# Window attention of a two-layer transformer: scores per head on 64x64 quarters of TensorE, two blocks of queries stacked per tile

## The chip, the cores and the metric

One core of a Trainium2 chip runs the whole program. The metric is device time in microseconds (us) of one execution. TensorE multiplies matrices (in the profile PE is its matmuls and PEld its weight loads), VectorE (DVE) and ScalarE (ACT) do elementwise work and read PSUM, GpSimd (POOL) does elementwise work on SBUF, and SyncE (SP) starts most transfers. Every engine runs its own queue in order; semaphores connect the queues.

## The reference

Two transformer layers with modulated norms over x of shape (4, 1024, 128). Each has an attention and a routed mixture of experts. The change is in the attention of the first layer: 16 heads of size 64, q and k with an RMS norm over all heads, a bias that is linear in the distance, and a causal window of 64 keys back.

```python
q = rmsnorm(x @ wq.T, q_norm_w); k = rmsnorm(x @ wk.T, k_norm_w); v = x @ wv.T   # split into 16 heads of 64
scores = einsum('bhqd,bhkd->bhqk', q, k) * HD ** (-0.5)
scores = scores + slopes[:, None, None] * dist               # dist = key position - query position
causal = (dist > 0) | (dist < -WINDOW)                       # WINDOW = 64
weights = softmax(where(causal, -inf, scores))
out = einsum('bhqk,bhkd->bhqd', weights, v) @ wo.T
...
h = layernorm(x) * (1 + ca) + sa                             # six modulation vectors for each batch element
x = x + ga * attention(h, ...)
h = layernorm(x) * (1 + cb) + sb
x = x + gb * experts(h, ...)
```

## The kernel before

The program goes through stages one after the other, with a barrier between them: `start_stage` (norm of x, modulation), `rms_stage`, `window_attention_stage` (the first layer's attention, with the routing of the experts for the first three batch elements woven in), `route_last_stage`, the first layer's experts, and then the second layer.

The attention works on pairs of heads: 4 batch elements with 8 pairs each make 32 pairs (`HP`). Queries come in blocks of 64 (`BLK`), so 1024 tokens are 16 blocks (`NBLK`), and each block of queries sees 128 keys: its own block and the one ahead of it. A group is four blocks, so a pair has four groups (`GRP`) and the stage 128 (`G`). All of it is float32. TensorE's 32-bit matmuls stand in the trace as two records each, each with its own weight load.

For the pair after the one that is being worked on, six units make q (units 0 and 1), k (2 and 3) and v (4 and 5), each of 512 tokens (`project`, L714 and L717), into two PSUM banks that alternate. They are copied out by ACT: k to `k_pad` (L824), v to `v_tiles` (L826). Of q, ACT writes head 0's half (L819) and DVE head 1's half (L892) into a block-diagonal `q_bd`: per block a 128x128 square with the two heads' queries on the diagonal and zeros elsewhere. The v tiles are also moved by 64 rows with two SP transfers into `v_shift`, since odd blocks begin at half a tile.

For each group, in order: one 128x128 matmul a block makes the scores of both heads, partitions 0 to 63 for one and 64 to 127 for the other (L734); DVE adds the bias and takes the minimum of the negated scores (L960); ACT takes the exponential and its row sum (L869), DVE inverts the sums (L966), POOL multiplies (L989), TensorE transposes (L745), DVE copies the result out (L972), TensorE multiplies with v, 128 rows by 64 columns of the array for each head (`o_ps`, L760), and ACT copies that out (L877). After the four groups of a pair, eight matmuls add its part of the output projection (`wo_ps`, L773). Two score banks alternate by group.

TensorE's order in step g is written out by hand: the scores of group g; the units of the next pair that fall into this step; the transposes of group g-2; the product of group g-3; every fourth step the output projection. The other engines have loops of their own over g, and the norms, logits, softmax and ranks of the router are hung in at fixed places within a batch element (the constants `STATS1` to `PREFIX`, counted in groups).

`start_stage` also makes six modulation vectors for each layer and batch element as rows, stores them to DRAM and loads them back into all partitions as `mod_rows` (P, 2, B, 6, D).

Of the kernel before, what the change touches and what calls it, by code (L numbers as in the profile page):

```python
# [21 lines left out]
P = 128  # L22
# [14 lines left out]
RMS_EPS = 1e-6  # L37

# [12 lines left out]
STATS1, HAT1, MODULATE, HAT2, TURN0, TURN1, LOGITS, SOFTMAX, PREFIX = 6, 9, 11, 16, 18, 19, 22, 23, 30  # L51
# [13 lines left out]
SA, CA, GA, SB, CB, GB = range(6)  # L65

# [122 lines left out]
def double_norm_stage(nc, K, A, name, layer, scale, shift, arrays, before=None):  # L189
# [3 lines left out]
    with ExitStack() as st:  # L193
# [9 lines left out]
        with nc.Block() as block:  # L203
# [7 lines left out]
            def _(dve):  # L211
# [9 lines left out]
                def modulate(b):  # L221

                    if b >= B:
# [4 lines left out]
                    nc.vector.tensor_tensor(h, h, bc(K.mod_rows[:, layer, b, scale, :], 1, TPB), ALU.mult  # L228
# [3 lines left out]
                                            bc(K.mod_rows[:, layer, b, shift, :], 1, TPB), ALU.add  # L232
# [48 lines left out]
def start_stage(nc, K, A, gram):  # L281
# [4 lines left out]
    rows_dram = nc.dram_tensor("mod_rows_dram", [2 * B * 6 * D], F32, kind="Internal").ap()  # L286
    with ExitStack() as st:
# [24 lines left out]
        with nc.Block() as block:  # L312
            @block.sync
            def _(sp):
# [10 lines left out]
                sp.dma_start(rows_dram.rearrange("(l b n) -> b l n", l=2, b=B), rows[:]).then_inc(rows_stored, 16)  # L325
# [242 lines left out]
def window_attention_stage(nc, K, A, gram, hq, hk, M, N1, N2, aff_in):  # L568
# [3 lines left out]
    with ExitStack() as st:  # L572
# [4 lines left out]
        nbias = K.sb("nbias", [P, PAIRS, P], ctx=st)  # L577
# [3 lines left out]
        qbd = K.sb("q_bd", [P, 2, NBLK, P], ctx=st)  # L581
# [14 lines left out]
        def fill(pool):  # L596

            for n, dst in enumerate((qbd[:].rearrange("p a b c -> p (a b c)"), kk[:, :, 0:BLK], vs[0:BLK, :, 0, :])):
                nc.gpsimd.memset(dst, 0.0).then_inc(filled, 1)
                pool.wait_ge(filled, n + 1)  # L600
            nc.gpsimd.memset(zero[:], 0.0).then_inc(filled, 1)
# [9 lines left out]
        def scale_q(dve):  # L611
# [19 lines left out]
        op = K.ps("o_ps", [P, 4, BLK], st)  # L631
        wp = [K.ps(f"wo_ps{i}", [P, CPT, D], st) for i in range(2)]
        (h_in, p_mm, a_out, q_out, v_sh0, v_sh1, s_mm, biased, exped, rsum, normed, turned, pt_out, pv_mm, o_out,
         wo_mm, wo_gated, x_added, prob_set, scaled, shifted) = K.sems(
            st, "win", "h_in", "proj_mm", "act_out", "q_out", "v_shift_even", "v_shift_odd", "score_mm", "biased",
            "exp", "rsum", "normed", "turned", "probsT_out", "pv_mm", "o_out", "wo_mm", "wo_gated", "x_added", "probs_set",
            "scaled", "shifted")
        v_sh = (v_sh0, v_sh1)
        GRP = NBLK // 4
        HP = B * PAIRS  # L640
        G = HP * GRP
        PER = GRP * PAIRS
        extra = {PER * (b + 1) + at: (b, what) for b in range(B - 1)
                 for at, what in ((TURN0, "turn0"), (TURN1, "turn1"), (LOGITS, "logits"), (PREFIX, "prefix"))}
        units = [(0, u) for u in range(6)]
        steps = []
        for g in range(G):
            h, start = g // GRP + 1, len(units)
            if h < HP:
                units += [(h, u) for u in ((0, 1), (2, 3), (4,), (5,))[g % GRP]]  # L650
            if g in extra:
                units.append(extra[g])
            steps.append(range(start, len(units)))
        place = {unit: n for n, unit in enumerate(units)}

        def unit_steps(g):

            return steps[g] if g < G else []

# [9 lines left out]
        with nc.Block() as block:  # L669
            @block.tensor  # L670
            def _(pe):
# [24 lines left out]
                def project(n):  # L696
# [3 lines left out]
                    if n >= 2:  # L700

                        hh, uu = units[n - 2]
                        pe.wait_ge(a_out, n - 1)
                        if uu in (0, 1):
                            pe.wait_ge(q_out, 2 * hh + uu + 1)
# [15 lines left out]

                for n in range(6):
                    project(n)
                for g in range(G + 4):
                    h, r = divmod(g, GRP)
                    if g < G:
                        if r == 0:
                            pe.wait_ge(a_out, out_count(h, 3))
                            pe.wait_ge(q_out, 2 * h + 2)
                        if g >= 2:  # L730
                            pe.wait_ge(biased, g - 1)
# [4 lines left out]
                        m.then_inc(s_mm, 1)  # L736
                    for n in unit_steps(g):
                        project(n)
                    if 2 <= g < G + 2:
                        k = g - 2  # L740
                        pe.wait_ge(normed, k + 1)
                        if k >= 1:
                            pe.wait_ge(pt_out, k)
                        for i in range(4):
                            m = nc.tensor.transpose(tp[:, i, :], pr[:, k % 3, i, :], K.ident[:])  # L745
                        m.then_inc(turned, 1)
                    if 3 <= g < G + 3:
                        k = g - 3
                        hh, rr = divmod(k, GRP)
                        pe.wait_ge(pt_out, k + 1)  # L750
                        if rr == 0:
                            pe.wait_ge(a_out, out_count(hh, 5))
                            pe.wait_ge(v_sh[hh % 2], 32 * (hh // 2 + 1))
# [1809 lines left out]
```

## Time and profile before

| | us |
|---|---|
| median of 3 runs | 2059.05 |
| lowest and highest | 2058.75 and 2061.07 |
| span of the profiled execution | 2056.4 |
| TensorE busy in it | 1579.5 |
| DVE busy | 1339.0 |
| ACT busy | 1135.7 |
| POOL busy | 550.2 |

The median lies 2.65 us above the span of the profiled execution. The busy times are sums over stages with different limits, so each stage is read by itself. In a timeline, records of the same kind that follow each other are merged: "x8" are eight records, and the next row's start tells when the following work began. A matmul's end is modelled, so the pace of TensorE is read from starts.

### The profile page before, as it was taken

The numbers are of one execution on the slowest core, as the hardware profiler recorded it, in microseconds if no ns is written. First come the engines' busy times: TensorE is split into PE (matmuls) and PEld (weight loads), VectorE is DVE, ScalarE is ACT, GpSimd is POOL, SyncE is SP. The second block draws the span as 40 slices with busy tenths as digits, with TensorE's granted clock in tenths as the row PEclk, the third lists the DMA queues.
The fourth block names the chain that finished last, engine by engine and source line by source line (L and its number), as shares of the span: only waits on it lengthen the run. The fifth ranks groups of instructions, "written<-read, shape, count | busy, mean of one in ns | idle before, by whom it ended". The sixth has DMA issues, their size and how long they took to land. (4 is left out here: it accounts for less than half of the span.)

```text
span 2056.4 us, 34421 instructions
## 1 busy us (share of the span) xinstructions
PE 1579.5 (77%) x11512; PEld 917.7 (45%) x11512; DVE 1339.0 (65%) x3318; ACT 1135.7 (55%) x2965; POOL 550.2 (27%) x615
## 2 busy tenths in 40 slices
PE   6799999999991699245999999999999735424910
PEld 3478777777771699221222222222222234323910
DVE  5655656656564322267999999999999287842523
ACT  3366766666651344142688888888888733111300
POOL 2133323524526400571001001001000020372056
PEclk9799999999995799666899999999999967556965
DMA  5144311211101676142000000000000000013832
GB/s 191 39 156 156 107 30 36 54 28 43 42 21 37 203 234 205 52 122 83 23 21 26 18 26 18 27 18 26 19 25 2 1 0 6 21 45 124 253 91 72
DMA packets 86203, 138.99 MB, mean 68 GB/s; under 512 B 18084, under 2 KB 57252, under 8 KB 85900
## 3 DMA queue, kind: packets, MB, share of 16 engines
q1 hardware_dynamic: 62860, 92.08, 15.2%
q0 software_dynamic: 11936, 34.49, 5.1%
q10 hardware_dynamic: 11232, 10.23, 1.4%
q8 instruction: 93, 1.52, 0.3%
q14 instruction: 82, 0.67, 0.1%
HBM read 75.51 MB, written 45.11 MB: 59 GB/s over the span
## 5 line engine op out<-in xcount | busy, mean ns | idle before, releaser
L2062 DVE TENSOR_REDUCE q_max<-s_ps 128x1 f32<-128x1024 f32 x512 | 598.2, 1219 | 14.0 <-PE s_ps L1953 6.8
L2043 ACT ACTIVATE probs<-s_ps 128x512 f32<-128x512 f32 x1024 | 535.5, 603 | 124.5 <-PE s_ps L1974 124.3
L1953 PE MATMUL s_ps<-k_stack,q_stack 64*128 64x512 bf16 x1024 | 351.2, 397 | 16.9 <-PEq L96 8.5
L1974 PE MATMUL s_ps<-q_stack,k_stack 64*128 64x512 bf16 x1024 | 319.5, 384 | 20.2 <-ACT probs L2043 15.8
L1988 PE MATMUL o_ps<-probs,v_aug 128*32 128x512 f32 x2048 | 273.6, 606 | 0.7 <-ACT probs L2043 0.7
L1974 PEld LDWEIGHTS s_ps<-q_stack,k_stack 64*128 64x128 bf16 x1024 | 78.6, 94 | 333.9 <-ACT probs L2043 281.9
L989 POOL TENSOR_TENSOR probs<-probs,p_rsum 128x512 f32<-128x512 f32 x128 | 132.9, 1038 | 325.8 <-DVE p_rsum L966 325.1
L869 ACT ACTIVATE probs<-s_biased,s_min 128x128 f32<-128x128 f32 (+1 forms) x512 | 197.7, 391 | 37.0 <-DVE s_min L960 35.6
L734 PE MATMUL score_ps<-k_pad,q_bd 128*128 128x128 f32 x1024 | 146.7, 287 | 0.0
L960 DVE CUSTOM_DVE_ANT_0 s_biased<-score_ps,nbias 128x128 f32<-128x128 f32 (+1 forms) x512 | 115.8, 282 | 41.8 <-PE score_ps L734 40.6
L1580 POOL CAST neg_max_parts<-neg_max 16x128 bf16<-16x128 f32 x32 | 9.0, 281 | 474.7 <-DVE neg_max L2070 474.7
L734 PEld LDWEIGHTS score_ps<-k_pad,q_bd 128*128 128x128 f32 x1024 | 125.9, 194 | 7.4 <-issue 1.0
L1953 PEld LDWEIGHTS s_ps<-k_stack,q_stack 64*128 64x128 bf16 x1024 | 77.5, 94 | 113.2 <-DVE q_max L2062 104.3
L892 DVE TENSOR_SCALAR q_bd<-proj_ps,qscale 64x512 f32<-64x512 f32 x64 | 48.4, 756 | 107.9 <-PE proj_ps L714 104.7
L1474 ACT ACTIVATE moe0b_hid<-moe0b_hps,moe0b_wblock 128x256 f32<-128x256 f32 x156 | 66.9, 473 | 82.5 <-PE moe0b_hps L1429 80.7
L972 DVE COPY probsT<-probsT_ps 128x512 f32<-128x512 f32 x128 | 86.7, 677 | 37.0 <-PE probsT_ps L745 36.4
L1619 POOL DMA_INDIRECT moe0g_yg<-moe_rows,moe_slot x64 | 66.4, 1038 | 157.9 <-POOLq L96 139.0
L869 ACT ACTIVATION_READ_ACCUMULATOR probs<-s_biased,s_min 128x1 f32 x512 | 98.0, 191 | 0.0
L1538 POOL DMA_INDIRECT moe1g_yg<-moe_rows,moe_slot x64 | 61.2, 956 | 121.3 <-PEq L1533 102.1
L819 ACT ACTIVATE q_bd<-proj_ps,qscale 64x512 f32<-64x512 f32 x64 | 43.7, 683 | 84.9 <-PE proj_ps L714 84.8
L1498 DVE TENSOR_TENSOR moe0b_y<-moe0b_yps,moe0b_wblock 128x256 f32<-128x256 f32 x39 | 16.6, 425 | 99.6 <-PE moe0b_yps L1439 99.6
L760 PE MATMUL o_ps<-probsT,v_shift 128*64 128x64 f32 x1024 | 73.5, 235 | 8.8 <-ACT oT L877 8.6
(315 smaller groups left out, 2824.5 us busy)
## 6 DMA issues: line engine op xcount, KB each, us to landing
moe0b_wblock<-in_L_ffn_blocks SPq DMA_DIRECT2D x39, 578.0 KB, 3.9
moe_rows<-zero_rows POOLq DMA_DIRECT2D x18, 960.0 KB, 4.4
moe1b_wblock<-in_L_ffn_blocks SPq DMA_DIRECT2D x39, 256.0 KB, 3.5
v_shift<-v_tiles SPq DMA_DIRECT2D x32, 256.0 KB, 3.1
v_shift<-v_tiles SPq DMA_DIRECT2D x32, 224.0 KB, 3.6
qk_parts_dram<-qk_parts SPq DMA_DIRECT2D x16, 384.0 KB, 2.7
q_stack<-qk_parts_dram SPq DMA_DIRECT2D x192, 32.0 KB
k_stack<-qk_parts_dram SPq DMA_DIRECT2D x192, 32.0 KB
```

What stands on the lines that cost most here:

```text
L734: m = nc.tensor.matmul(sp_[g % 2][:, i, :], qbd[:, h % 2, j, :], kk[:, h % 2, BLK * j:BLK * j + P], start=True, stop=True)
L760: m = nc.tensor.matmul(op[a * BLK:(a + 1) * BLK, i, :], src[:, a * HD0:(a + 1) * HD0], pt[:, k % 2, i, a * BLK:(a + 1) * BLK], start=True, ...
L869: r = nc.scalar.activation(pr[:, g % 3, i, own], sb_[:, g % 2, i, own], ACT.Exp, scale=-1.0, bias=mn[:, g % 4, i:i + 1], accum_out=sm[:, g ...
L960: q = v.tensor_tensor_reduce(sb_[:, g % 2, i, own], sp_[g % 2][:, i, own], nbias[:, h % PAIRS, own], 1.0, 3e38, ALU.add, ALU.min, mn[:, g ...
L972: v.tensor_copy(pt[:, k % 2], tp[:]).then_inc(pt_out, 1)
L989: nc.gpsimd.tensor_tensor(pb, pb, bc(ri[:, g % 4, :], 2, P), ALU.mult).then_inc(normed, 1)
L1474: nc.scalar.activation(hid[:, j % 2, f, :], hp[n % 4][:, 0:BR], gelu, bias=bias).then_inc(g_out, 1)
L1953: mm = nc.tensor.matmul(s1[u % 2][:, c * CH:(c + 1) * CH], qs[head_rows(m), quad % 4, j, qt * P:(qt + 1) * P], ks[head_rows(m), quad % 4, ...
L1974: nc.tensor.matmul(bank_of("exp", 4 * k + pos)[:], ks[head_rows(m), quad % 4, j, kt * P:(kt + 1) * P], qs[head_rows(m), quad % 4, j, half ...
L1988: m = nc.tensor.matmul(op[32 * h:32 * h + 32, :], va[:, quad % 2, kt, h, :], pr[:, k % 2, h, :], start=(kt == 0), stop=(kt == TPB - 1))
L2043: nc.scalar.activation(pr[:, k % 2, HEADS[pos], :], bank_of("exp", n)[:], ACT.Exp).then_inc(sm["exp"], 1)
L2062: v.tensor_reduce(mx[:, h % 4, col:col + 1], s1[u % 2][:], AX.X, ALU.max).then_inc(sm["maxed"], 1)
```

## The change

- Scores: `q_bd` is replaced by `q_rows`, q of both heads as it comes (128 rows, 1024 columns a pair). A block's score of one head is a matmul of 64 rows by 64 columns of the array, which are the quarters (row half a = the head, column half e = even or odd block). Bank a now holds head a alone, with an even block on partitions 0 to 63 and the odd one on 64 to 127.
- Steps: a step is eight blocks, with both banks; a pair has two steps (`HALVES`), the stage 64 (`S`). Transposes, probabilities and copies keep their size (four tiles of 128x128) but belong to one head; there are two a step, g = 2n and 2n+1. The product of a step is taken at once, for both heads (`o_ps` has 512 columns). Units come three in each step.
- ACT writes q out alone, 128 partitions at a time; DVE's half is gone, and its clearing of `probs` too. The first block of each sequence has no block ahead of it: its 64 columns get FAR added by two small matmuls for each head (`outside`).
- Buffers: `probs` has four in place of three, `probsT` four in place of two; the bias is kept for all 16 heads on all partitions (1024 KB in place of 512 KB).
- `mod_rows` keeps four kinds of rows out of six (from GA on).
- The router's prefix is placed two groups earlier.

```diff
+ROW0 = GA
-    rows_dram = nc.dram_tensor("mod_rows_dram", [2 * B * 6 * D], F32, kind="Internal").ap()
+    rows_dram = nc.dram_tensor("mod_rows_dram", [2 * B * (6 - ROW0) * D], F32, kind="Internal").ap()
...
-        nbias = K.sb("nbias", [P, PAIRS, P], ctx=st)
+        nbias = K.sb("nbias", [P, H0, P], ctx=st)
-        qbd = K.sb("q_bd", [P, 2, NBLK, P], ctx=st)
+        qq = K.sb("q_rows", [P, 2, T], ctx=st)
+        outside = K.sb("outside", [P, BLK], ctx=st)
...
-        pr = K.sb("probs", [P, 3, 4, P], ctx=st)
+        pr = K.sb("probs", [P, 4, 4, P], ctx=st)
-        pt = K.sb("probsT", [P, 2, 4, P], ctx=st)
+        pt = K.sb("probsT", [P, 4, 4, P], ctx=st)
-        op = K.ps("o_ps", [P, 4, BLK], st)
+        op = K.ps("o_ps", [P, 8, BLK], st)
...
-                units += [(h, u) for u in ((0, 1), (2, 3), (4,), (5,))[g % GRP]]
+                units += [(h, u) for u in ((0, 1, 2), (3, 4, 5))[n % HALVES]]
...
+                def scores(n):
+                    h, r = divmod(n, HALVES)
+                    if r == 0:
+                        pe.wait_ge(a_out, out_count(h, 3))
...
+                    if n >= 1:
+                        pe.wait_ge(biased, 2 * n)
+                    for i in range(4):
+                        edge = r == 0 and i == 0
+                        for e, a in ((0, 0), (1, 1), (1, 0), (0, 1)):
+                            j, rows = 8 * r + 2 * i + e, slice(a * BLK, (a + 1) * BLK)
+                            m = nc.tensor.matmul(sp_[a][e * BLK:(e + 1) * BLK, i, :],
+                                                 qq[rows, h % 2, BLK * j:BLK * (j + 1)],
+                                                 kk[rows, h % 2, BLK * j:BLK * j + P],
+                                                 start=True, stop=not (edge and e == 0))
+                        if edge:
+                            for a in range(2):
+                                rows = slice(a * BLK, (a + 1) * BLK)
+                                m = nc.tensor.matmul(sp_[a][0:BLK, 0, 0:BLK], M.ones[rows, 0:BLK], outside[rows, :],
+                                                     start=False, stop=True)
+                    m.then_inc(s_mm, 1)
...
-                for g in range(G + 4):
-                        for i in range(4):
-                            j = 4 * r + i
-                            m = nc.tensor.matmul(sp_[g % 2][:, i, :], qbd[:, h % 2, j, :],
-                                                 kk[:, h % 2, BLK * j:BLK * j + P], start=True, stop=True)
...
+                for n in range(S + 3):
+                    mine = list(own(n))
+                    if n < S:
+                        scores(n)
+                    for k in mine[:2]:
+                        project(k)
+                    if 1 <= n < S + 1:
+                        turn(2 * (n - 1))
+                    if 2 <= n < S + 2:
+                        product(n - 2)
+                    for k in mine[2:]:
+                        project(k)
+                    if 1 <= n < S + 1:
+                        turn(2 * (n - 1) + 1)
+                    if n >= 4 and n % HALVES == 0:
+                        output_product((n - 4) // HALVES)
+                    for k in extra(n):
+                        project(k)
...
             @block.scalar
...
+                for n in range(S + 2):
+                    mine = list(own(n))
+                    for k in mine[:1]:
+                        evacuate(k)
+                    if n < S:
+                        exponentials(2 * n)
+                    for k in mine[1:2]:
+                        evacuate(k)
+                    if n < S:
+                        exponentials(2 * n + 1)
+                    for k in mine[2:]:
+                        evacuate(k)
...
+                    if n >= 2:
+                        output(n - 2)
...
             @block.vector
...
-                    v.tensor_scalar(qbd[BLK:P, h % 2, u * 8:u * 8 + 8, BLK:P],
-                                    pj[n % 2][BLK:P, :].rearrange("p (j q) -> p j q", q=BLK),
-                                    qs[BLK:P, h % PAIRS:h % PAIRS + 1], None, ALU.mult).then_inc(q_out, 1)
...
+                for n in range(S + 1):
+                    if n < S:
+                        bias(2 * n)
+                        bias(2 * n + 1)
+                    if n >= 1:
+                        turned_out(2 * (n - 1))
+                    if n < S:
+                        invert(2 * n)
+                    if n >= 1:
+                        turned_out(2 * (n - 1) + 1)
+                    if n < S:
+                        invert(2 * n + 1)
+                    routed(2 * n)
+                    routed(2 * n + 1)
```

## Rows read from the trace of the kernel before

**Rows 1.** Windows, first to last pair's scores: us; PE, PEld, DVE, ACT, POOL busy; PEclk; DMA.
```profile
87.10:597.20 510.10, 493.88 (x4723) 399.84 (x4722) 306.70 (x1507) 350.76 (x1344) 193.85 (x182) 0.99 0.23 71
```
**Rows 2.** Waits in 87 to 618 us: line, releaser, us in total, times, longest.
```profile
PE o_ps L760 <- ACT oT L877: 8.6, 28, 0.7
PE proj_ps L680 <- issue: 6.3, 3, 2.1
```
**Rows 3.** Timeline of PE (start, us, line): first and last pair's first scores.
```profile
87.10 1.05 PE L734 MATMUL score_ps<-k_pad,q_bd 128*128 128x128 f32 x8
...
597.20 1.06 PE L734 MATMUL score_ps<-k_pad,q_bd 128*128 128x128 f32 x8
```
**Rows 4.** Timeline of PE, each kind of work of one pair.
```profile
331.49 1.16 PE L734 MATMUL score_ps<-k_pad,q_bd 128*128 128x128 f32 x8
332.48 1.88 PE L714 MATMUL proj_ps<-hk,wkT 128*128 128x512 f32 x4
334.20 0.60 PE L745 MATMUL probsT_ps<-ident,probs 128*128 128x128 f32 x4
334.73 0.33 PE L760 MATMUL o_ps<-probsT,v_shift 128*64 128x64 f32 x4
334.89 0.29 PE L760 MATMUL o_ps<-probsT,v_tiles 128*64 128x64 f32 x4
335.01 0.29 PE L760 MATMUL o_ps<-probsT,v_shift 128*64 128x64 f32 x4
...
335.35 1.16 PE L734 MATMUL score_ps<-k_pad,q_bd 128*128 128x128 f32 x8
336.34 1.06 PE L717 MATMUL proj_ps<-wvT,nat 128*128 128x128 f32 x8
337.23 0.33 PE L692 MATMUL proj_ps<-moe_chosen,moe_before 128*128 128x64 f32 x2
...
342.59 2.05 PE L773 MATMUL wo_ps<-woT_gated,oT 128*128 128x128 f32 x16
344.48 1.06 PE L734 MATMUL score_ps<-k_pad,q_bd 128*128 128x128 f32 x8
```
**Rows 5.** Timeline of PE in the second layer's attention: quarter columns, then half rows.
```profile
1299.50 1.06 PE L1988 MATMUL o_ps<-probs,v_aug 128*32 128x512 f32 x8
1300.49 0.39 PE L1974 MATMUL s_ps<-q_stack,k_stack 64*128 64x512 bf16 x1
1300.50 0.39 PE L1953 MATMUL s_ps<-k_stack,q_stack 64*128 64x512 bf16 x1
1300.72 0.38 PE L1974 MATMUL s_ps<-q_stack,k_stack 64*128 64x512 bf16 x1
```
**Rows 6.** Groups of ACT by line, 237 to 366 us: busy us, mean ns, idle.
```profile
L869 ACT ACTIVATE probs<-s_biased,s_min 128x128 f32<-128x128 f32 x116 | 45.1, 393 | 1.7 <-DVE s_min L960 1.3 <-ACT moe_raw L795 0.2 <-ACT moe_totals L800 0.2
L819 ACT ACTIVATE q_bd<-proj_ps,qscale 64x512 f32<-64x512 f32 x16 | 10.9, 683 | 18.9 <-PE proj_ps L714 18.9
L877 ACT COPY oT<-o_ps 128x256 f32<-128x256 f32 x30 | 10.6, 353 | 0.0
L826 ACT COPY v_tiles<-proj_ps 128x512 f32<-128x512 f32 x15 | 8.7, 581 | 12.3 <-issue 12.3
```
**Rows 7.** The same for DVE and POOL.
```profile
L960 DVE CUSTOM_DVE_ANT_0 s_biased<-score_ps,nbias 128x128 f32<-128x128 f32 x112 | 26.0, 286 | 8.0 <-PE score_ps L734 7.9
L972 DVE COPY probsT<-probsT_ps 128x512 f32<-128x512 f32 x30 | 20.2, 674 | 9.0 <-PE probsT_ps L745 8.8
L989 POOL TENSOR_TENSOR probs<-probs,p_rsum 128x512 f32<-128x512 f32 x31 | 32.2, 1039 | 90.8 <-DVE p_rsum L966 90.8
```
**Rows 8.** First stage: transfers view (KB, us to landing), then timeline rows.
```profile
mod_rows<-mod_rows_dram SPq DMA_DIRECT2D x1, 3072.0 KB, 9.5
...
22.87 0.36 SPq L327 DMA_DIRECT2D mod_rows<-mod_rows_dram  x1
33.65 0.37 ACT L374 COPY gram<-gram_ps 128x256 f32<-128x256 f32 x1
```

More of the change, by code:

```diff
@@ L37 @@
 RMS_EPS = 1e-6
+FAR = 1e30
 E = 8
@@ L637, in window_attention_stage @@
             "scaled", "shifted")
         v_sh = (v_sh0, v_sh1)
-        GRP = NBLK // 4
+        HALVES = 2
         HP = B * PAIRS
[L641 to L644, printed above, removed]
+        S = HP * HALVES
+        PER = 2 * HALVES * PAIRS
         units = [(0, u) for u in range(6)]
-        steps = []
-        for g in range(G):
-            h, start = g // GRP + 1, len(units)
+        own_units, extra_units = [], []
@@ L649, in window_attention_stage @@
+        for n in range(S):
+            h, start = n // HALVES + 1, len(units)
             if h < HP:
-                units += [(h, u) for u in ((0, 1), (2, 3), (4,), (5,))[g % GRP]]
-            if g in extra:
-                units.append(extra[g])
-            steps.append(range(start, len(units)))
+                units += [(h, u) for u in ((0, 1, 2), (3, 4, 5))[n % HALVES]]
+            own_units.append(range(start, len(units)))
+            b, at = n // (PER // 2) - 1, 2 * (n % (PER // 2))
+            start = len(units)
+            if b >= 0:
+                units += [(b, what) for when, what in ((TURN0, "turn0"), (TURN1, "turn1"), (LOGITS, "logits"),
+                                                       (PREFIX, "prefix")) if when in (at, at + 1)]
+            extra_units.append(range(start, len(units)))
@@ new lines, in output_product @@
+                def output_product(hh):
+                    pe.wait_ge(o_out, HALVES * (hh + 1))
+                    bb, hw = divmod(hh, PAIRS)
+                    if hw == 0:
+                        pe.wait_ge(wo_gated, bb + 1)
+                        if bb >= 1:
+                            pe.wait_ge(x_added, 2 * bb)
+                    for t in range(TPB):
+                        m = nc.tensor.matmul(wp[t // CPT][:, t % CPT, :], oT[:, hh % 2, t * P:(t + 1) * P],
+                                             wog[:, hw, :], start=(hw == 0 and t % CPT == 0),
+                                             stop=(hw == PAIRS - 1), skip_group_check=True)
+                    m.then_inc(wo_mm, 1)
@@ L834, in copy_tokens, with exponentials, output @@
                     nc.scalar.copy(hb[b % 2], K.hT[:, b * T:(b + 1) * T]).then_inc(h_in, 1)
+                def exponentials(g):
+                    act.wait_ge(biased, g + 1)
+                    if g >= 4:
+                        act.wait_ge(turned, g - 3)
+                    for i in range(4):
+                        r = nc.scalar.activation(pr[:, g % 4, i, :], sb_[:, g % 2, i, :], ACT.Exp, scale=-1.0,
+                                                 bias=mn[:, g % 4, i:i + 1], accum_out=sm[:, g % 4, i:i + 1])
+                    r.then_inc(exped, 1)
+                def output(k):
+                    act.wait_ge(pv_mm, k + 1)
+                    hh, r = divmod(k, HALVES)
+                    if r == 0 and hh >= 2:
+                        act.wait_ge(wo_mm, hh - 1)
+                    nc.scalar.copy(oT[:, hh % 2, r * CH:(r + 1) * CH], op[:].rearrange("p j q -> p (j q)")
+                                   ).then_inc(o_out, 1)
                 def routed(g):
@@ L937, in routed @@
                         M.weights(dve, b)
[L938 removed]
+                    elif at == PREFIX + 2:
                         M.place(dve, b, M.raw[:])
@@ new lines, in bias @@
+                def bias(g):
+                    n, a = divmod(g, 2)
+                    dve.wait_ge(s_mm, n + 1)
+                    if g >= 2:
+                        dve.wait_ge(exped, g - 1)
+                    head = 2 * (n // HALVES % PAIRS) + a
+                    for i in range(4):
+                        q = v.tensor_tensor_reduce(sb_[:, a, i, :], sp_[a][:, i, :], nbias[:, head, :], 1.0, 3e38,
+                                                   ALU.add, ALU.min, mn[:, g % 4, i:i + 1])
+                    q.then_inc(biased, 1)
```

228 lines of the change are left out of this document (81 added, 147 removed).

## The prediction

> **What bounds the kernel now.** I read the stage of the change first, by its own window: from the first pair's scores at 87.10 us to the last pair's at 597.20 us [rows 3] TensorE is busy for 493.9 of 510.1 us, DVE for 306.7, ACT for 350.8 and POOL for 193.9, at a granted clock of 0.99, which is the 2.4 GHz level [rows 1]. The other three have a third or more of the time left, so TensorE's queue sets the pace. Next I read the waits: TensorE's largest are 8.6 us for ACT's copy of the product's bank and 6.3 us ahead of the router's transposes [rows 2]. Last I read one pair in the timeline, from start to start, because a matmul's end overlaps the next [rows 4].
>
> The price list of a pair comes from there. Eight full-array records of 128 columns take 0.89 us (v, 336.34 to 337.23), 0.111 each. Two 512-column units take 1.72 (332.48 to 334.20), 0.86 each. Four transposes take 0.53 when the product comes next, that is 0.44 at the same 0.111 each and 0.09 for the switch. The product, which splits the array into two column halves, takes 0.62 for 16 records (334.73 to 335.35); four of them start every 0.12 (334.89 to 335.01), so 0.48 is pace and 0.14 is getting in and out. The scores after it take 0.99 (335.35 to 336.34) in place of 0.89. A visit to the split array thus costs 0.14 + 0.09 + 0.10 = 0.33 besides its records. The output projection takes 1.89 (342.59 to 344.48), of which 0.10 belongs to the product ahead of it.
>
> Sum of a pair now: scores 4 x 0.89 = 3.56, products 4 x (0.48 + 0.33) = 3.24, q and k 4 x 0.86 = 3.44, v 2 x 0.89 = 1.78, transposes 4 x 0.44 = 1.76, output 1.79: 15.57 us. The 31 pairs between the two starts [rows 3] make 482.7; the remaining 27.4 of the 510.1 are the router's own matmuls and the waits.
>
> **The change part by part.**
>
> Scores. A block's 128x128 matmul was half zeros. Now each head's block is one 64x64 quarter with the same 128 columns to stream, 16 such matmuls a step, four to each quarter. If the quarters run at the same time, a step costs the eight records of one quarter, 8 x 0.111 = 0.89, plus 0.33 for the visit: 1.22. In every first step of a pair one quarter of each bank gets a 64-column matmul more, two records at 0.06 (four records in two halves every 0.12): 1.34. A pair: 2.56, where 3.56 stood.
>
> The trace of before has no 64x64 matmul, so this is bounded from its neighbours. Columns: four tiles of 32 columns finish eight records of 512 columns in 0.99 us (1299.50 to 1300.49), where one unit of two such records takes 0.86 alone on the full array [rows 4, 5]; four tiles at once, two records of one matmul behind each other in each. Rows: two matmuls of 64 rows start 0.01 us apart and the next one 0.22 later [rows 5]; two at once, in different banks. The change needs both together and keeps a head to its own bank. Lower end: no switch to pay at the scores' own visits, 0.89 a step. Upper end: nothing at once, 16 x 2 x 0.111 = 3.55 a step. I take the four at once, since each half of it stands in rows, and keep the others as rivals.
>
> Products. The same records in half as many visits: 2 x (32 x 0.03 + 0.33) = 2.58, where 3.24 stood. Visits to the split array stay four in a pair: four products before, two products and two scores after.
>
> Everything else on TensorE stays. New pair: 2.56 + 2.58 + 3.44 + 1.78 + 1.76 + 1.79 = 13.91, less by 1.66; over 31 pairs 51.5 us.
>
> The waits. The 8.6 us for ACT's copy go: a step's product now needs the copy of the step before, which by the walk below ends 1.8 us or more ahead. The 6.3 us ahead of the router's transposes go too, as they come at the end of a step, some 6 us after the norm they wait for is due. That leaves 27.4 - 14.9 = 12.5. For new ones I put 7, so 19.5 (bounds 12.5 and 27.4): the router's DVE pieces are hung behind the steps' own work as before, but now in lumps of two places.
>
> ACT. It took 350.8 / 31 = 11.3 us a pair with all router work [rows 1]. q keeps its two writes (0.683, now on 128 partitions in place of 64; k and v at 128 partitions take 0.58, so I see no reason for more); the output copies are two of twice the width, by v's row 2 x 0.58 in place of 4 x 0.353 [rows 6], 0.25 less: 11.1 of 13.9. DVE loses its half of q and keeps bias (0.232 a tile by busy time), inverse and copies (0.674); POOL's 1.039 a group stays [rows 7]. Both stay below ACT.
>
> Where does the order make them wait? A first step is 1.34 + 1.72 + 0.44 + 1.29 + 0.86 + 0.44 + 1.79 = 7.88, a second 1.22 + 0.86 + 0.89 + 0.44 + 1.29 + 0.89 + 0.44 = 6.03. ACT begins a first step with q's half, projected 2.2 in (1.34 + 0.86), then four exponentials (4 x 0.393), the other half, four more, k and the output: done near 8.0. In the second step k is projected at 9.96, ACT goes on then and is done near 15.5, 1.6 into the next first step and 0.6 before it gets work there. The nearest need of TensorE is v's second bank, copied near 14.9 and wanted by q's second unit at 13.9 + 2.2 = 16.1. So ACT fits, with about 1 us to spare once a pair and more elsewhere. DVE copies the second transposes after 13.9 until 14.6 and starts the next bias at 15.2.
>
> Edits with one answer, cost nothing: the modulation rows (3072 KB became 2048) landed at 22.87 + 9.5 = 32.4, ahead of ACT's last copy, whose end at 34.0 closes that stage [rows 8]; were that copy gone, the smaller transfer would save up to 3 us. The bias table's 512 KB more, by the same row under 2 us, is covered by the 50 us of other work up to 87.10 [rows 3]; without the cover it would cost those 2. The cleared `q_bd` and DVE's clearing lie off the path, and so does the shift of v on SP, asked for a step or more ahead of the product. Ramp and last pair: the first scores wait for the same four copies on ACT, and the last pair has two longer steps in place of four; I take 0, bounds 3 either way.
>
> Sum: 510.1 - (31 x 13.91 + 19.5) = 510.1 - 450.7 = 59.4 less. The profiled span of 2056.4 becomes 1997.0; the median of the runs lies 2.65 above it, so 1999.6.
>
> **The rivals.**
>
> ACT sets the second steps. ACT's share grows from 0.69 to 0.80, and its slack of 1 us is worked out from means. If TensorE's second steps (6.03) stretch half way to the first ones (7.88), 0.92 a pair, 28.5 us come back: 2028. Against it: ACT idles over 2 us after each first step. Chance 0.14.
>
> Weight loads don't hide. Each record has a load of its own, and a quarter's next load has the same rows as its running matmul. In the product's visits the loads hide or cost little: a half takes a load and a 64-column record every 0.06 us [rows 4]. If each of the eight records of a quarter paid up to that 0.06, a step costs 0.48 more, a pair 0.96: 29.8 us, 2029. Chance 0.07. The Trainium skill, "TensorE: Matmul & The Clock Gate", Part 3, under what overlaps, says that a load runs beside a matmul in flight only when their row groups differ, which would make this the case here; the product's rows, whose matmuls all use the same 128 rows, speak against it.
>
 Chance 0.06.
>
> Slower: quarters run one by one, where row halves and column halves don't mix. A step costs 3.55 + 0.33, a first one 0.24 more: 8.0 a pair in place of 2.56, 31 x 5.44 = 168.6 more against the 59.4 saved (66.4 without the new waits, as all other engines then have time): 2161. It decides from 59.4 / 62 = 0.96 us a step on, at about 2.2 us a step. Chance 0.05. The Trainium skill, "TensorEngine Tiling (Array Packing)", Gotcha 1, says that different row tiles can't use one PSUM bank at the same time, which would bring half of this rival for scores in one bank; here each row half has its own, and no run here shows the other.
>
> **How the numbers follow.** Forecast as summed: 0.68, with its own range 1980 to 2018: below, no switch cost at the scores (2 x 0.33 x 31 = 20 us); above, all 27.4 us of waits kept, the edges of ramp and tail, and some ACT stalls. Up to 2038 the first two rivals come in, 0.89 in all less the outskirts; the other 0.11 are left out. What a measurement tells from no change is about 0.2%, 4 us. Faster: 0.68 + 0.14 + 0.07, rounded down to 0.88; the two-at-once rival lies on the border and counts as the same; slower 0.06.
>
> **What would show it.** The pair's period on TensorE near 14.5 us with all waits (510.1 / 31 = 16.5 now); score records starting eight in 0.22 us, four quarters by two, a step's visit near 1.2; ACT busy over three quarters of the stage, waiting for projections and hardly waited for; the product's wait for ACT nearly gone. Wrong, if a step's scores take 2 us or more, if TensorE waits for ACT's copies for over 1 us a pair, or if a stage outside this one moves by over 3 us.

## The result, and the profile after

| | before, us | after, us |
|---|---|---|
| median of the runs | 2059.05 | 2005.62 (2004.87 to 2005.89) |
| span of the profiled execution | 2056.4 | 2003.6 |
| first pair's to last pair's scores | 510.10 | 447.72 |
| last pair's first scores to the end of the stage | 20.96 | 29.48 |

The ratio after to before is 0.9738, with a 95% interval of 0.9725 to 0.9752: 53.4 us less, where 59.4 were forecast. The end of the stage is the end of the last residual addition on DVE, 618.16 us before and 562.55 after.

The windows of the changed kernel (us; busy PE, PEld, DVE, ACT, POOL; granted clock; DMA): first to last pair's scores, then the last pair in two parts, cut at its second step's scores. The first line answers [rows 1].

```profile
85.35:533.07 447.72, 435.73 (x5805) 335.19 (x5804) 269.67 (x1439) 343.29 (x1278) 194.23 (x182) 1.00 0.27 80
533.07:544.47 11.40, 7.04 (x97) 6.48 (x96) 9.89 (x35) 5.37 (x23) 3.48 (x3) 0.85 0.18 45
544.47:562.55 18.08, 13.40 (x177) 11.80 (x176) 8.50 (x32) 5.15 (x21) 2.08 (x2) 0.81 0.00 1
```

TensorE still bounds the stage between the pairs, at full granted clock, and ACT is now busy for 0.77 of it. A pair takes 447.72 / 31 = 14.44 us with all waits, where 14.5 was named. The tail is another matter: TensorE is busy for 20.4 of 29.5 us, and the granted clock is 0.85 and 0.81. These are means over stretches at either level. Windows cut where the clock changes show two stretches at 0.50, the 1.2 GHz level, 10.2 us together; the tail of the kernel before, below them, has none.

```profile
539.80:543.21 3.41, 2.82 (x14) 2.85 (x15) 2.28 (x7) 2.69 (x13) 1.88 (x2) 0.50 0.02 5
550.04:556.86 6.82, 6.04 (x53) 5.55 (x52) 3.63 (x9) 0.91 (x2) 1.04 (x1) 0.50 0.01 2
```
```profile
597.20:618.16 20.96, 16.61 (x206) 14.31 (x204) 13.16 (x60) 8.89 (x41) 5.20 (x5) 1.00 0.05 14
```

TensorE's timeline over one undisturbed pair (start, us, line), which answers [rows 4]: scores are L742, the first block's edge L749 (one matmul for each head, two records), q and k L720, v L723, transposes L759, the product L775, the output projection L791.

```profile
324.89 0.45 PE L742 MATMUL score_ps<-k_pad,q_rows 64*64 64x128 f32 x8
...
326.04 1.98 PE L720 MATMUL proj_ps<-hq,wqT 128*128 128x512 f32 x4
327.86 0.60 PE L759 MATMUL probsT_ps<-ident,probs 128*128 128x128 f32 x4
328.39 0.34 PE L775 MATMUL o_ps<-probsT,v_shift 128*64 128x64 f32 x4
...
329.47 1.12 PE L720 MATMUL proj_ps<-hk,wkT 128*128 128x512 f32 x2
330.43 0.60 PE L759 MATMUL probsT_ps<-ident,probs 128*128 128x128 f32 x4
330.87 1.95 PE L791 MATMUL wo_ps<-woT_gated,oT 128*128 128x128 f32 x16
332.75 1.10 PE L742 MATMUL score_ps<-k_pad,q_rows 64*64 64x128 f32 x32
333.78 1.13 PE L720 MATMUL proj_ps<-hk,wkT 128*128 128x512 f32 x2
334.75 1.05 PE L723 MATMUL proj_ps<-wvT,nat 128*128 128x128 f32 x8
...
338.77 0.45 PE L742 MATMUL score_ps<-k_pad,q_rows 64*64 64x128 f32 x8
```

Read from start to start: a first step takes 332.75 - 324.89 = 7.86 us, a second one 338.77 - 332.75 = 6.02, a pair 13.88. The 32 records of a second step's scores take 1.03 us (332.75 to 333.78). Single records of such a visit start in fours: 333.018, 333.025, 333.032, 333.038, and the next four from 333.128. Four quarters run at once, each at the 0.11 us that a full-array record of 128 columns takes.

The waits from 85 to 563 us (line, releaser, us in total, times, longest) answer [rows 2]; below them is the first line again for the time between the first and the last pair's scores alone:

```profile
PE probsT_ps L759 <- DVE probsT L1007: 13.4, 12, 4.3
PE proj_ps L690 <- ACT v_tiles L863: 2.3, 3, 0.8
```
```profile
PE probsT_ps L759 <- DVE probsT L1007: 7.3, 9, 1.6
```

TensorE's wait for ACT's copy of the product is gone. In its place TensorE waits for DVE's copies of the turned probabilities, twelve times; 7.3 us of the 13.4 lie between the pairs, and 6.1, with the longest of 4.3, in the last pair.

### The profile page after: what moved, and what is told of

Read it like the earlier page. It is cut to its first block and busy times, and to the rows that moved or that the text cites. A ratio compares the mean times of both kernels' runs of the same rounds, so it can differ in the third digit from the quotient of the medians.

```text
span 2003.6 us, 36434 instructions
## 1 busy us (share of the span) xinstructions
PE 1529.1 (76%) x12664; PEld 858.7 (43%) x12664; DVE 1305.7 (65%) x3253; ACT 1130.1 (56%) x2901; POOL 547.0 (27%) x615
## 5 line engine op out<-in xcount | busy, mean ns | idle before, releaser
L879 ACT ACTIVATE probs<-s_biased,s_min 128x128 f32<-128x128 f32 x512 | 198.6, 391 | 31.7 <-DVE s_min L993 31.1
L993 DVE CUSTOM_DVE_ANT_0 s_biased<-score_ps,nbias 128x128 f32<-128x128 f32 x512 | 113.0, 285 | 46.6 <-PE score_ps L742 46.4
L759 PE MATMUL probsT_ps<-ident,probs 128*128 128x128 f32 x512 | 78.6, 277 | 14.4 <-DVE probsT L1007 13.4
L759 PEld LDWEIGHTS probsT_ps<-ident,probs 128*128 128x128 f32 x512 | 61.4, 142 | 50.1 <-issue 48.4
L1490 PEld LDWEIGHTS moe0b_yps<-moe0b_wblock,moe0b_hid 128*128 128x128 f32 x624 | 75.6, 192 | 2.0
L1480 PE MATMUL moe0b_hps<-moe0b_xT,moe0b_wblock 128*128 128x256 f32 x312 | 76.0, 388 | 0.0
L1490 PE MATMUL moe0b_yps<-moe0b_wblock,moe0b_hid 128*128 128x128 f32 x624 | 75.8, 275 | 0.0
```

The source lines that it names most:

```text
L759: m = nc.tensor.transpose(tp[:, i, :], pr[:, g % 4, i, :], K.ident[:])
L879: r = nc.scalar.activation(pr[:, g % 4, i, :], sb_[:, g % 2, i, :], ACT.Exp, scale=-1.0, bias=mn[:, g % 4, i:i + 1], accum_out=sm[:, g % 4 ...
L993: q = v.tensor_tensor_reduce(sb_[:, a, i, :], sp_[a][:, i, :], nbias[:, head, :], 1.0, 3e38, ALU.add, ALU.min, mn[:, g % 4, i:i + 1])
L1490: m = nc.tensor.matmul(yp[j % 2][:, a * P:(a + 1) * P], hid[:, j % 2, f, a * P:(a + 1) * P], wb[:, j % WBUF, F + f * D:F + (f + 1) * D], s ...
```

## The experiments

The kernel before was run beside each group: 2059.8 us beside the first four, 2057.46 beside the next three, 2057.5 beside the three after them and 2056.64 beside the last. Ratios go by these.

**1. Every score matmul twice.** Does a step's visit cost what four quarters at once would make it cost, and does TensorE set the pace?

```
-  for e, a in ((0, 0), (1, 1), (1, 0), (0, 1)):
+  for n_, (e, a) in enumerate(((0, 0), (1, 1), (1, 0), (0, 1)) * 2):
       ...  start=True, stop=not (edge and e == 0 and n_ >= 4))
```

> The changed kernel with each quarter's score matmul issued twice; the second one overwrites the first, so nothing of the result changes. Theory (TensorE's queue sets the stage, four quarters at once): each step's visit grows by eight more records of one quarter, 8 x 0.111 = 0.89 us, 62 steps on the path, 55 us: about 2061 us; score records still four wide. Rival (ACT or the chain of the step now sets the pace and TensorE has slack): under 25 us, below 2031. Rival (quarters share something and run two at a time): 1.78 us a step more, 2116.

Measured: 2053.39 us, ratio 0.9971 (0.9958 to 0.9983). TensorE's timeline, a second step's scores and what follows them:

```profile
330.65 1.98 PE L742 MATMUL score_ps<-k_pad,q_rows 64*64 64x128 f32 x64
332.56 0.70 PE L720 MATMUL proj_ps<-hk,wkT 128*128 128x512 f32 x1
```

The second set of 32 records costs 1.91 - 1.03 = 0.88 us, eight records of 0.11. Undisturbed steps are 8.74 and 6.90 us, 0.88 more each, so ACT doesn't set a second step even part of the way. The time from first to last pair grows by 45.3 us and not by 62 x 0.88 = 54.6, and the time stays below the 2061 of the theory: in steps that the router disturbs, the longer scores run within a wait (TensorE's waits for DVE between the pairs fall from 7.3 to 1.5 us). Weight loads hide: the added records cost their columns and no more. The rule of the Trainium skill ("TensorE: Matmul & The Clock Gate", Part 3, on what overlaps), by which a load overlaps a matmul in flight only in another row group, would have shown here as more than 0.11 a record, as a quarter's next load has the rows of its own running matmul. The measurement decides against that rule taken by itself.

**2. One quarter after the other.** The same matmuls, with the four of a quarter issued together.

```
-  for i in range(4):
-      for e, a in ((0, 0), (1, 1), (1, 0), (0, 1)):
+  for e, a in ((0, 0), (1, 1), (1, 0), (0, 1)):
+      for i in range(4):
...
```

> The changed kernel with the order of a step's score matmuls turned: all four of one quarter first, then the next quarter. The same matmuls. Theory A (each quarter has a stream of its own, and the queue looks far enough ahead to fill it): a step's visit stays 1.0 to 1.2 us, 2005 us. Theory B (matmuls start in the order of the queue, and the even spread over quarters in the changed kernel is what makes four at once): the four streams run one behind the other, up to 3.55 us a step in place of 0.89, 62 x 2.66 = 165 us more, 2170; something between where the queue looks ahead part of the way.

Measured: 2087.35 us, ratio 1.0141 (1.0124 to 1.0158), slower than the kernel before. TensorE's timeline, the same place:

```profile
329.91 2.56 PE L742 MATMUL score_ps<-k_pad,q_rows 64*64 64x128 f32 x32
332.40 1.12 PE L720 MATMUL proj_ps<-hk,wkT 128*128 128x512 f32 x2
```

The visit takes 2.49 us in place of 1.03. Single records show why. They start at 329.907, 330.067, 330.176, 330.285 and 330.394; then a second series begins at 330.400, between which the first goes on, at its pace of 0.11, at 330.503, 330.612 and 330.722. Further series begin at 330.893 and 331.387. The records don't name their quarter, but four series of eight fit (the first record of each is shown as 320 ns long, the others as 269): a quarter begins 0.49 us after the one before it, when three of that one's eight records are left, so two run together at most. Both theories were off in size: it is neither full overlap nor none. The gain of the change thus hangs on the order in which it issues its matmuls.

**3. Column halves alone.** Steps of eight blocks and one head a bank as in the change, but q padded with zeros again, so that each matmul uses 128 rows and 64 columns. ACT writes q in two pieces, into rows that were cleared once.

```
-  qq = K.sb("q_rows", [P, 2, T], ctx=st)
+  qq = K.sb("q_rows", [P, 2, 2, T], ctx=st)
...
-  qq[rows, h % 2, BLK * j:BLK * (j + 1)], kk[rows, h % 2, BLK * j:BLK * j + P],
+  qq[:, h % 2, a, BLK * j:BLK * (j + 1)], kk[:, h % 2, BLK * j:BLK * j + P],
```

> The changed kernel with its steps of eight blocks and one head a bank, but scores on column halves over all 128 rows: q is kept per head with zeros in the other head's rows (two ACT writes of 64 partitions a unit in place of one), so two matmuls at a time in place of four. The rows to be cleared are written from a smaller tile for want of space. Theory (the gain is the scores' time on the array): a step's visit grows by 0.89 to about 2.1 us, 62 steps, 55 us: 2060. Rival (the gain came from longer steps, half as many product visits and fewer waits): below 2030.

Measured: 2058.94 us, ratio 0.9993 (0.9983 to 1.0003).

```profile
336.69 1.97 PE L742 MATMUL score_ps<-k_pad,q_rows 128*64 128x128 f32 x32
338.58 1.12 PE L720 MATMUL proj_ps<-hk,wkT 128*128 128x512 f32 x2
```

In this timeline the visit takes 1.89 us and a pair 8.84 + 6.89 = 15.73, next to the 15.84 of before. So the new steps, banks and buffers by themselves bring nothing that the time shows. But that nothing is a gain and a loss, as the windows show (first to last pair's scores, then the tail):

```profile
88.68:587.82 499.14, 492.36 (x5806) 394.20 (x5805) 270.99 (x1439) 398.55 (x1340) 199.40 (x182) 1.00 0.27 72
587.82:616.56 28.74, 19.65 (x273) 17.71 (x272) 18.39 (x66) 10.53 (x44) 5.56 (x5) 0.94 0.07 18
```

Between the pairs the new steps save 11.0 us (499.14 for 510.10), and in the tail they lose 7.8 (28.74 for 20.96). Of the 62.4 us that the change saves between the pairs, the other 51.4 (447.72 for 499.14) are the scores' time on the array. The longer tail comes with the steps, not with the quarters.

**4. Modulation rows alone.** The kernel before with four kinds of rows stored and loaded.

```
-  sp.dma_start(rows_dram..., rows[:]).then_inc(rows_stored, 16)
+  sp.dma_start(rows_dram..., rows[:, :, ROW0 * D:]).then_inc(rows_stored, 16)
...
```

> The kernel before with one part of the change alone: four kinds of modulation rows kept in place of six. Theory: the transfer lands earlier, but ACT's last copy closes that stage; no change, 2059 within 2 us. Rival: up to 3 us faster where the transfer closed the stage or slowed others.

Measured: 2059.33 us, ratio 0.9999 (0.9990 to 1.0009): nothing.

**5. The output copied twice.** ACT gets 0.58 us more in every step, on the rival that ACT is near to setting the second steps.

```
   def output(k):
+      nc.scalar.copy(spare[:], op[:].rearrange("p j q -> p (j q)"))
```

> The changed kernel with one more copy of the product's bank on ACT in each step, into a spare tile: 0.58 us more ACT work a step, 1.16 a pair, everything else as it is. Theory (TensorE sets the undisturbed step, ACT has about 1 us to spare in a pair at its tightest place and more elsewhere): a pair's undisturbed period of 13.89 grows by 0.3 at most; 2006 to 2014 us. Rival (ACT all but sets the second steps): 31 x 1.16 = 36 us more, 2041.

Measured: 2007.0 us, ratio 0.9752 (0.9737 to 0.9767). The groups of ACT by line (busy us, mean ns, idle) show that the work was done, and TensorE's timeline that a pair didn't notice:

```profile
L890 ACT COPY spare<-o_ps 128x512 f32<-128x512 f32 x8 | 4.7, 584 | 0.0
```
```profile
327.60 0.45 PE L743 MATMUL score_ps<-k_pad,q_rows 64*64 64x128 f32 x8
...
335.46 1.10 PE L743 MATMUL score_ps<-k_pad,q_rows 64*64 64x128 f32 x32
...
341.49 0.45 PE L743 MATMUL score_ps<-k_pad,q_rows 64*64 64x128 f32 x8
```

7.86 and 6.03 us again. One ACT write of 0.58 us a step, 1.17 a pair, fits into the slack, so that rival falls.

**6. Router pieces between the two halves of a step.** In the change DVE does the router's pieces of both places behind the second copy of the turned probabilities, and the next step's bias waits behind them. Here the first place's pieces go ahead of that copy.

```
       invert(2 * n)
+  routed(2 * n)
   if n >= 1:
       turned_out(2 * (n - 1) + 1)
...
-  routed(2 * n)
   routed(2 * n + 1)
```

> The changed kernel with half of the router's DVE pieces (those of the even places) put between the two halves of a step, ahead of the copy of the second transposes, where DVE waits for TensorE, in place of the step's end. Theory (what disturbs the steps is DVE coming late to the next bias after two pieces in a row): the places with long steps shrink, 9.2 to about 8.0 (place 6 of 16), 10.06 to about 8.5 (place 14), some tenths at places 0 and 4, for three batch elements 10 us, and 2 us in the last pair: 1993 us. Rival (the long steps come from ACT or from the chain through POOL): 2003 to 2006.

Measured: 1998.65 us, ratio 0.9711 (0.9698 to 0.9724). A disturbed step on TensorE in the changed kernel, then the same step here: its scores, its second transposes, the next step's scores.

```profile
294.55 0.45 PE L742 MATMUL score_ps<-k_pad,q_rows 64*64 64x128 f32 x8
...
301.87 0.63 PE L759 MATMUL probsT_ps<-ident,probs 128*128 128x128 f32 x4 [1.61 <-DVE probsT L1007]
304.61 1.10 PE L742 MATMUL score_ps<-k_pad,q_rows 64*64 64x128 f32 x32
```
```profile
295.55 0.45 PE L742 MATMUL score_ps<-k_pad,q_rows 64*64 64x128 f32 x8
...
301.79 0.63 PE L759 MATMUL probsT_ps<-ident,probs 128*128 128x128 f32 x4 [0.53 <-DVE probsT L1007]
304.53 1.10 PE L742 MATMUL score_ps<-k_pad,q_rows 64*64 64x128 f32 x32
```

The step falls from 10.06 to 8.98 us as TensorE's wait for DVE falls from 1.61 to 0.53. First to last pair takes 441.76 us, 6.0 less; the tail, 29.60, doesn't move. The direction was as expected, the size wasn't: 10 us and 2 in the last pair were put, and 1993 in all.

**7. Later turns.** The sixth kernel, with the router's two transposes one step later (places 20 and 21 in place of 18 and 19).

```
-  ..., TURN0, TURN1, ... = ..., 18, 19, ...
+  ..., TURN0, TURN1, ... = ..., 20, 21, ...
```

> As the run with the router's pieces put between, and the router's transposes on TensorE moved from the end of a second step (place 9) to the end of a first one (place 10), where the projection banks they use have been copied out. Theory: the wait of 0.8 us ahead of them goes, three times, 2.4 us less than that run. Rival: nothing, or they hold up the next step's first units for as long.

Measured: 1994.83 us, ratio 0.9698 (0.9684 to 0.9711). Place 9 of a batch element's sixteen steps falls from 7.90 to 6.02 us, place 10 rises from 7.86 to 8.74: first to last pair 438.75, 3.0 us less than in the sixth.

**8. The last choice left out.** Where do the tail's 8.5 us come from? The routed batch element beside the last pairs takes the choice of the one before it.

```
   elif at == SOFTMAX + 3:
-      M.compare(dve)
+      if b < B - 2:
+          M.compare(dve)
   elif at == SOFTMAX + 4:
-      M.order(dve)
+      if b < B - 2:
+          M.order(dve)
+      else:
+          dve.sem_inc(M.chose, 1)
```

> Leaves out, for the one batch element whose experts are chosen beside the last pairs, the comparison and the ordering of its probabilities (six VectorE instructions, 0.66 + 1.53 + 0.42 + 0.42 + 0.69 + 0.20 us in the changed kernel); that batch element takes the choice of the one before it. The changed kernel's last pair needs 29.48 us from its first scores to the end of the stage, 8.5 more than the kernel before. Theory: these instructions stand on VectorE ahead of the last pair's bias (from 533.97 to 537.95), so the first step of that pair takes 11.40 instead of 7.86 us and TensorE then waits 4.3 us and runs on at a lower granted clock. Then this step falls to 7.5 to 8, the tail to 23 to 25.5, the granted clock of the tail goes back towards 1.00, and the time is about 2000 (1998 to 2002). Rival: the tail grew behind the last scores, through the order of the last products; then the step falls but the tail stays at 28 us or more by waiting later, and the time is 2004 to 2006.

First the changed kernel. DVE's timeline, last pair (its first scores start at 533.07): six router instructions stand ahead of the first bias. Below it TensorE's, over the same stretch.

```profile
533.97 0.66 DVE L1288 TENSOR_TENSOR moe_gt<-moe_pb 128x512 bf16<-128x512 f32 x1
534.54 1.53 DVE L1289 TENSOR_TENSOR moe_eq<-moe_pb 128x512 bf16<-128x512 f32 x1
...
537.75 0.20 DVE L1298 TENSOR_SCALAR moe_chosen<-moe_rank 128x64 f32<-128x64 f32 x1
537.87 0.29 DVE L993 CUSTOM_DVE_ANT_0 s_biased<-score_ps,nbias 128x128 f32<-128x128 f32 x1
```
```profile
540.39 1.09 PE L759 MATMUL probsT_ps<-ident,probs 128*128 128x128 f32 x4 [4.31 <-DVE probsT L1007]
541.27 2.88 PE L791 MATMUL wo_ps<-woT_gated,oT 128*128 128x128 f32 x16
543.99 0.33 PE L702 MATMUL proj_ps<-moe_chosen,moe_before 128*128 128x64 f32 x2
```

After the wait of 4.31 us the output projection takes 2.72 us (541.27 to 543.99) where it takes 1.88 in an undisturbed pair: up to 543.21 the granted clock is 0.50. Without the six instructions (windows, the last pair in two parts, columns as above):

```profile
533.69:540.24 6.55, 5.69 (x97) 5.14 (x96) 5.17 (x25) 5.37 (x23) 2.90 (x3) 1.00 0.32 79
540.24:556.91 16.67, 11.88 (x177) 10.28 (x176) 9.63 (x36) 5.15 (x21) 2.29 (x3) 0.90 0.01 1
```

The tail is 23.23 us, 6.25 less; its first step falls from 11.40 to 6.55, by more than forecast, as the last pair's steps hold no projections for a next pair, and the granted clock stays at 1.00 there; the 0.90 of the second part holds one stretch at 0.50, of 3.41 us. The time is 1998.44 us, ratio 0.9714 (0.9699 to 0.9729). The rival falls.

**9. Another order at the end.** The changed kernel with two edits in the last steps: the last product on TensorE ahead of the last but one pair's output projection, and DVE's placing behind the last copies.

```
   if n >= 4 and n % HALVES == 0:
-      output_product((n - 4) // HALVES)
+      if n < S or n == S + 2:
+          output_product((n - 4) // HALVES)
+  if n == S + 1:
+      output_product(S // HALVES - 2)
...
-  elif at == PREFIX + 2:
+  elif at == PREFIX + 2 and b < B - 2:
       M.place(dve, b, M.raw[:])
...
+  if n == S:
+      M.place(dve, B - 2, M.raw[:])
```

> The changed kernel with another order at the very end: TensorE issues the last product ahead of the last but one pair's output product (16 matmuls, 3.23 us), and VectorE does the placing of the last routed batch element (550.02 to 552.38) behind the last two copies of the turned probabilities. Theory that the end is a chain through these two: the last copy is 2.4 us earlier, the last product no longer stands behind the output product, and the time from the last step's scores (544.47) to the end of the stage falls from 18.1 to 14 to 16 us; the time is about 2003 (2001 to 2004.5). Theory that the tail is lost ahead of the last scores alone: 18.1 stays within 1 us and the time stays at 2005 to 2006.

Measured: 2000.75 us, ratio 0.9727 (0.9712 to 0.9743), which isn't told apart from the change's 0.9738 (0.9725 to 0.9752). In its profile the part from the last scores on is 16.14 us, 1.9 less than the change's 18.08, a little less of a gain than the 2 us that were the least expected.

**10. The seventh kernel with that end.** The edits of 6, 7 and 9 together.

> Router pieces between the two halves of a step and later turns (the version that took 1994.8), with the same other order at the end. If both edits add up: 1991 to 1993. If the end is off the path there (its tail is 28.42 us, of which the placing holds the second last copy 2.35 us): 1994 to 1995.5.

Measured: 1991.51 us, ratio 0.9679 (0.9662 to 0.9696), the lowest median of all; the interval overlaps the seventh kernel's. Its tail is 26.52 us, 1.9 less than the seventh's 28.42. The last stretch at 0.50 is equally long in these two profiles (3.42 us in the seventh, 3.41 here), so this gain isn't the clock's.

**11. Both edits of the tail.** The edits of 8 and 9 together.

> Both edits of the tail together: the last routed batch element's comparison and ordering left out (it takes the choice of the one before it), the last product ahead of the last but one pair's output product, and the placing behind the last copies. Alone they made the tail 23.23 and 27.52 us, where the changed kernel has 29.48 and the kernel before 20.96. If the tail's growth is these two and nothing else, they add up: 29.48 - 6.25 - 1.96 = 21.3, within 0.7 us, and about 1995 to 1997 us. If both removed the same wait (the second edit's gain being only the fallen clock's), the tail stays at 22.5 to 23.2, and some 2 us of the growth have another cause, such as the last step being twice as long.

Measured: 1997.19 us, ratio 0.9707 (0.9691 to 0.9723), and from the windows:

```profile
534.69:541.25 6.56, 5.71 (x98) 5.15 (x97) 5.16 (x25) 5.38 (x23) 2.90 (x3) 1.00 0.32 79
541.25:557.68 16.43, 12.12 (x177) 10.51 (x176) 8.88 (x36) 5.16 (x21) 2.29 (x3) 0.90 0.01 1
```

The tail is 22.99 us, so the two don't add up: beside the eighth the other order brings 0.2 us. It helped where the last pair's first step came late (experiments 9 and 10) and hardly where that is mended; why is not shown. Of the 8.5 us, 6.25 are the six router instructions with what they cause, 0.2 the order, and 2.0 (22.99 for 20.96) have another cause. That this is the length of the last step, eight blocks with nothing beside them where there were four, fits the waits in it, but no run halved that step, so it stays argued. The clock has a part in it: in this tail TensorE is busy all through a stretch of 3.42 us at 0.50, and the tail of before has none; at full clock that work would take some 1.7 us less, by my estimate from the stretch's length.

Not tried was a kernel with both heads in one bank. The rule on banks that the prediction names beside its slower rival is left open by these runs.

## Why the prediction was right, and which term was off

The time came out 6.0 us above the forecast and in its own range. By the steps of the prediction:

- **A pair's work on TensorE: right.** 13.91 was summed and 13.88 measured, by steps 7.88 and 6.03 against 7.86 and 6.02. The pieces hold too: a second step's scores take 1.03 us, and the work on both sides of them runs some 0.10 longer than by itself (k 0.97 for 0.86, the output projection 1.88 for 1.79), which are the 0.33 of a visit besides its 0.89. The old pair, 15.57 by the price list, is 15.84 from start to start in the trace of before; the missing 0.27 is the wait for ACT's copy (8.6 / 31 = 0.28) [rows 2], which the sum kept among the waits. One reading slipped without effect: ACT had 0.31 of the stretch left, a little under the third that the prediction names.
- **Four at once: right**, by single records and by the first experiment. The rivals of two at once (2055) and one by one (2161) fall, as does that of the weight loads (2029). The second experiment came nearest to them: with the same matmuls in another order at most two quarters run together. The prediction didn't see that its price needs this order; by itself the term was right only because the change has it.
- **ACT's slack: right.** About 1 us a pair was worked out; 1.17 more a pair left the undisturbed steps as they were. That rival (2028) falls.
- **The waits: right in sum.** 447.72 - 31 x 13.88 = 17.4 us, where 19.5 were put. The wait for ACT's copy went, and router work in lumps of two places made new waits for DVE, as the prediction said: 7.3 us between the pairs, where 7 was put. As the 7 was put and not worked out, that nearness is luck. Of the 6.3 us ahead of the router's transposes, which were all to go, 2.3 stayed, now as waits for ACT's copy of v. Experiments 6 and 7 took 9.0 us away (447.72 to 438.75). The prediction also didn't see that about 2 us of the 510.10 were the clock's: behind two of those waits of 2.1 us the granted clock was 0.50 for 3.4 us (from 286.18 and from 555.83), and these two pairs took 20.65 and 20.70 us where the third took 19.67.
- **Modulation rows: right**, nothing. The first scores started at 85.35 us, 1.75 earlier than in the trace of before; in the profiles of the experiments with the new scores they start between 85.4 and 88.7, so I count nothing for the ramp.
- **The last pair: off.** It was put at 0, bounds 3, and it costs 8.5 us (20.96 to 29.48). The step that failed is "the last pair has two longer steps in place of four; I take 0": it looked at the length of the steps and not at what the lumps do there. Two places' pieces, compare and order, now run from 533.97 to 537.95 without a bias between them, where the kernel before had one between them (at 593.58). In the middle of the stage such a lump costs 10.06 - 7.86 = 2.2 us. In the last pair TensorE has no more projections to put beside it, waits 4.3 us, and comes back at a granted clock of 0.50. Experiment 8 shows that this is 6.25 of the 8.5 us. The prediction named no sign for this part: its last line speaks of stages outside this one, and the tail is inside.
- **Small losses elsewhere.** 62.4 us saved between the pairs, 1.75 at the start and -8.5 in the tail make 55.6 at the end of the stage; the spans differ by 52.8. The other 2.8 us come after the stage, where the profiles of before and after take 1438.2 and 1441.0 us. In the ten other profiles with the new steps this part takes 1436.5 to 1441.5, and in six of them less than 1439, so I count the 2.8 us to the execution and not to the change.

So of the 6.6 us between the spans (2003.6 for 1997.0), the tail's 8.5 and the later 2.8 stand against 3.0 more between the pairs than forecast (62.4 for 59.4) and 1.75 at the start.

## What to carry to other kernels

Price a tiled matmul by its records on one tile plus what a visit to the split array costs, both from rows of the same kernel, and issue the tiles in turn: grouped by tile, the same matmuls turned the gain into a loss. When a pipeline gets fewer and longer steps, look at the work that is hung behind a step, since it comes in larger lumps, and walk the last step by itself, where nothing runs beside the lump. Waits at a stage's end can cost more than their length: for 10.2 of the changed kernel's last 29.5 us the granted clock was 0.50.

## What the runs showed of the hardware

- Order of issue between tiles: quarters in turn start four records in 0.02 us and the next four 0.11 later; grouped by quarter, the next quarter starts 0.49 us after the one before it, 2.49 us a step for 1.03. The Trainium skill ("TensorE: Matmul & The Clock Gate", Part 3, on what overlaps) says that matmuls start and end strictly in program order. That they start late behind an occupied quarter agrees with it; that a series begins at 330.400, ahead of records at 330.503 to 330.722 that fit only the quarter issued before it, does not.
- The fall of the granted clock in the tail, from 1.00 to 0.50: first in the wait of 4.31 us, for 3.41 us, then behind waits of 1.02 and 0.87 us, for 6.82. The output projection in the first takes 2.72 us for 1.88. With the first wait removed the first part of the tail stays at 1.00. In the kernel before's tail, with waits of 0.89 us at most, the clock doesn't fall.
